# Attention blocks on one core: V weighed one block later, reciprocal sums turned after the projection, their copy after the exponentials

## The reference

```python
q, k, v = proj(Wq), proj(Wk), proj(Wv)           # 16 heads of 32
q, k = _apply_rope(q, cos, sin), _apply_rope(k, cos, sin)
scores = einsum('bhqd,bhkd->bhqk', q, k) / sqrt(32)
scores = where(causal, scores, finfo(float32).min)
attn = einsum('bhqk,bhkd->bhqd', softmax(scores), v)
x = x + layernorm(einsum('bsi,oi->bso', attn, Wo))
# then x = x + layernorm(experts(layernorm(x)))
```

## Time and profile before

| | |
|---|---|
| three runs | 1173.42, 1173.48, 1176.66 us |
| profiled execution: its own time, its span | 1176.2 us, 1174.3 us |
| the attention's blocks | from about 32 to 424 us of the span |
| PE busy over the span | 1080.3 us, 92% |
| DVE, ACT, POOL busy | 683.6, 483.4, 630.4 us |
| granted TensorE clock, mean | 0.975 |

### The profile page before, as it was taken

How to read it: one execution, slowest core, us unless ns; L and a number is a source line. 1 busy time by engine, 2 the same in 40 slices (tenths; PEclk the granted TensorE clock), 3 DMA queues, 4 the chain that set the end, 5 groups by cost and what they waited for, 6 DMA issues and landing times.

```text
span 1174.3 us, 24363 instructions
## 1 busy us (share of the span) xinstructions
PE 1080.3 (92%) x6281; PEld 726.1 (62%) x6282; DVE 683.6 (58%) x2349; ACT 483.4 (41%) x1357; POOL 630.4 (54%) x648
## 2 busy tenths in 40 slices
PE   6999899999999979988879999999999999999973
PEld 3555566555656546555547777777777777767631
DVE  5666566556666668868845444455444444545447
ACT  2666566656666644433212222222222222222223
POOL 3533333333333313321148788888888888888724
PEclk9999999999999999989979999999999999999987
DMA  8700000000000042100259999999999999997796
GB/s 315 287 2 1 3 1 1 2 2 1 1 2 2 1 187 91 63 19 19 72 177 212 222 198 252 248 234 240 260 232 250 243 229 277 272 226 148 110 334 240
DMA packets 66279, 166.71 MB, mean 142 GB/s; under 512 B 15379, under 2 KB 17171, under 8 KB 66081
## 3 DMA queue, kind: packets, MB, share of 16 engines
q0 software_dynamic: 38496, 83.95, 32.6%
q1 hardware_dynamic: 27712, 81.88, 19.7%
HBM read 119.85 MB, written 62.65 MB: 155 GB/s over the span
## 4 chain that ended last, share of the span: by engine, by line
PE 71%; DMA 12%; DVE 6%; issue 4%; ACT 2%; POOL 2%; POOLq 0%; DVEq 0%; SPq 0%; ACTq 0%
PE ps L956 15%; PE ps L700 15%; DMA sum_rows<-x_t,idx 8%; PE ps L967 8%; PE ps L759 6%; PE ps L817 4%; PE ps L729 4%; PE ps L940 4%; PE ps L779 4%; DMA x_t<-x_rows,idx 3%; PE ps L853 3%; PE ps L714 2%; PE ps L869 1%; PE ps L833 1%; POOL x_t L458 1%
## 5 line engine op out<-in xcount | busy, mean ns | idle before, releaser
L956 PE MATMUL ps<-big,work 128*128 x1264 | 300.5, 381 | 0.0
L464 POOL DMA_INDIRECT sum_rows<-x_t,idx x157 | 250.0, 1592 | 52.3 <-issue 40.2
L956 PEld LDWEIGHTS ps<-big,work 128*128 128x128 f32 x1264 | 229.0, 191 | 24.9
L458 POOL DMA_INDIRECT x_t<-x_rows,idx x159 | 166.2, 1045 | 63.5 <-issue 28.1
L700 PE MATMUL ps<-big 128*128 128x384 f32 x512 | 181.5, 499 | 2.1 <-ACT big L533 1.7
L384 POOL TENSOR_TENSOR work<-qkv_all,rope_sb 128x256 f32<-128x256 f32 x64 | 46.7, 729 | 245.2 <-ACT qkv_all L538 245.2
L654 ACT ACTIVATE work<-ps 128x512 f32<-128x512 f32 x159 | 95.0, 597 | 192.6 <-PE ps L940 131.6
L967 PE MATMUL ps<-big,work 128*128 x314 | 161.2, 595 | 1.8 <-issue 1.6
L940 PEld LDWEIGHTS ps<-ident_sb,x_t 128*128 128x128 f32 x636 | 78.7, 142 | 101.6 <-issue 71.0
L1061 DVE CUSTOM_DVE_ANT_0 ps<-ps,mask_sb 128x128 f32<-128x128 f32 (+3 forms) x256 | 120.6, 512 | 23.8 <-PE ps L729 23.0
L557 ACT ACTIVATE work<-ps,neg_max 128x128 f32<-128x128 f32 (+3 forms) x256 | 132.5, 528 | 3.3 <-DVE neg_max L1061 2.4
(11 more groups left out here) (177 smaller groups left out, 1459.9 us busy)
## 6 DMA issues: line engine op xcount, KB each, us to landing
big<-experts SPq DMA_DIRECT2D x65, 768.0 KB, 14.5
sum_rows<-x_t POOLq DMA_DIRECT2D x4, 2048.0 KB
big<-sum_rows SPq DMA_DIRECT2D x8, 768.0 KB, 9.5
x_rows<-work SPq DMA_DIRECT2D x16, 256.0 KB, 2.0
sum_rows<-attn_t POOLq DMA_DIRECT2D x2, 2048.0 KB
out<-x_sb SPq DMA_DIRECT2D x16, 256.0 KB, 5.2
x_sb<-x SPq DMA_DIRECT2D x3, 1024.0 KB, 10.2
x_t<-sum_rows SPq DMA_DIRECT2D x4, 768.0 KB, 13.1
```

The lines of the kernel that those rows point to most:

```text
L458: pool.indirect_dma_start(rows[:, q, :], None, x2_rows, bass.IndirectOffsetOnAxis(ap=idx[:, q, 0:1], axis=0), bounds_check=last_row, oob_i ...
L464: pool.indirect_dma_start(all_sums, bass.IndirectOffsetOnAxis(ap=idx[:, q, 1:2], axis=0), y_sb[:, q, :], None, bounds_check=last_sum, oob_ ...
L956: mm = pe.matmul(ps[:, 2 + p, 0:GATEUP], rows_t[:, p, c, :], w_ring[:, slot, c * GATEUP:(c + 1) * GATEUP], start=(c == 0), stop=(c == DC - 1))
```

## The change

Three things move, on three engines.

- PE: `weigh` of block k-1 now stands in block k between `score` and `xt` or `turn` of head 2. Only the last block of a sequence still weighs at its own end, so that block has two. `turn_rden` stands behind `proj`.
- ACT: `evac_rden` stands behind the exponentials and `evac_qkv`.
- DVE: `weighted` of block k-1 stands in block k behind `evac_pt`, between the second and the third `masked`; block 15's is where it was.

With them the waits change. From block 1 of a sequence on, `qkt` waits for `evac_rden` of the block before (`s_rden_t`), and for `weighted` of the block before that; and `weigh` waits for `take_qkt` of the same block.

```diff
 (ACT)
                     evac_pt(k, i, 2)
-                    evac_rden(k)
                     if i + 1 < BLOCKS or not last:
                         for h in range(HG):
                             exp(b * BLOCKS + (i + 1), (i + 1) % TB, h)
                     if i < BLOCKS - TB or not last:
                         evac_qkv(b * BLOCKS + (i + LEAD_PROJ), (i // TB + 1) % G, i % TB, qkv_bank)
+                    evac_rden(k)
 (PE)
-            def qkt(n, t, k):
+            def qkt(n, t, k, late=False, after=None):
                 pe.wait_ge(s_rope, n + 1)
+                if late:
+                    pe.wait_ge(s_rden_t, k)
+                    if after is not None:
+                        pe.wait_ge(s_attn, after)
...
-                if k is not None and not (isinstance(k, int) and k == 0):
+                if k is not None and not late and not (isinstance(k, int) and k == 0):
                     pe.wait_ge(s_attn, k)
...
-            def weigh(k, i):
+            def weigh(k, i, qkts):
...
                 pe.wait_ge(s_rden_t, k + 1)
+                pe.wait_ge(s_qkt, qkts)
...
                     if i + LEAD_QKT < BLOCKS or not last:
-                        qkt(b * BLOCKS + (i + LEAD_QKT), (i + LEAD_QKT) % TB, k)
+                        qkt(b * BLOCKS + (i + LEAD_QKT), (i + LEAD_QKT) % TB, k, late=(i >= 1),
+                            after=b * BLOCKS + (i - 1) if i >= 2 else None)
                     if i + 1 < BLOCKS or not last:
                         score(b * BLOCKS + (i + 1), (i + 1) % BLOCKS)
+                    if i >= 1:
+                        weigh(b * BLOCKS + (i - 1), i - 1, qkts)
...
                     turn(k, i, 3)
-                    turn_rden(k, b * BLOCKS + min(i + LEAD_QKT + 1, BLOCKS) if last else b * BLOCKS + (i + LEAD_QKT + 1))
                     if i < BLOCKS - TB or not last:
                         proj(b * BLOCKS + (i + LEAD_PROJ), (i // TB + 1) % G, i % TB, qkv_bank,
                              after_xt=(b + 1) * TB if i >= BLOCKS - TB else None)
-                    weigh(k, i)
+                    turn_rden(k, qkts)
+                weigh(b * BLOCKS + (BLOCKS - 1), BLOCKS - 1, qkts)
 (DVE)
                     evac_pt(k, i)
+                    if i >= 1:
+                        weighted(b, b * BLOCKS + (i - 1), i - 1)
                     if more:
                         masked(k1, q1, 2)
                         masked(k1, q1, 3)
-                    weighted(b, k, i)
+                    if i == BLOCKS - 1:
+                        weighted(b, k, i)
```

More of the change, by code:

```diff
@@ L787, in batch @@
                     k = b * BLOCKS + i
+                    qkts = b * BLOCKS + min(i + LEAD_QKT + 1, BLOCKS) if last else b * BLOCKS + (i + LEAD_QKT + 1)
                     turn(k, i, 0)
```

## The result

The changed kernel takes 1196.5 us (median of 6 runs, 1193.7 to 1197.3), the kernel before, run with it, 1174.2 us (6 runs). The ratio is 1.0174, 95% interval 1.0162 to 1.0187, which is 20.4 us (19 to 22); the two medians are 22.3 us apart, and the two profiled executions 20.4 (1196.64 and 1176.2 us). The forecast was +20.7.

The account below looks back on a forecast made before the run. PE was taken to set the pace, by its matmuls plus its standstills. Terms 11.8+3.7+2.2+2.0-1.1+1.0-0.9+2.0 gave +20.7 us on the 1173.5 us median, so 1194 us; own range 1183 to 1206, 8 in 10 1181 to 1207.

Parts of the forecast that it names:

- The main step: At `qkt`, PE newly waits for two queued ACT copies that `weigh` no longer covers; +1.02 us per four blocks in all.
- `norm_x`: On DVE, it follows the reciprocals ahead of `take_qkt` in four blocks of a looped sequence, delaying `weigh`: +2.0 us in all.
- the `xt` terms: At `xt`: its wait hidden by `weigh`, -1.1 us; `proj` behind it losing cover, +1.0; block 15's exponentials, -0.9.
- The prediction's check of blocks 20 to 22: This stretch, 17.23 us before the change, should take 17.8 us after it.
- `weigh` for `take_qkt`: Between `score` and `weigh`: a new wait of 0.17 us with scores of 128 columns, none with 256.
- The shape change: On PE: three tile-shape changes in a block instead of four, saving 0.09 us a block.
- the three sequence ends: Block 15 of each looped sequence: its `weigh` must wait for `evac_rden`, +0.8 us less some hiding, +2.2 in all.
- Behind the last projection: Last four blocks, without projection: `weigh` lies in the chain ahead of `turn`, +2.0 us (-2 to +4).
- The rival of the falling clock: New PE waits lower the clock once in every four blocks: +25 us on top, 1219 us; chance 3%.
- That nothing would replace the wait: At `qkt`, the old wait goes and both ACT copies finish in time: 1159 us; chance 5%.
- That it cancels: PE and ACT react faster than any row shows, leaving about no change: 1171 to 1179 us; chance 6%.
- That the exponentials become the bound beyond qt 3: ACT's exponentials come late by 0.4 us in qt 2 and 0 too: +12, 1206 us and over; chance 9%.

Follow-up runs that it names:

- Experiment 2: The changed kernel with the turned reciprocals in PSUM bank 7, beside the projection, instead of bank 6: 1176.0 us, ratio 1.000 to the kernel before.
- experiment 1: The changed kernel with `evac_rden` ahead of `evac_qkv` on ACT instead of behind it: 1186.8 us, ratio 1.010 to the kernel before.
- experiment 7: The kernel of experiment 2 with `invert` behind `take_qkt` on DVE instead of ahead of it: 1164.3 us, ratio 0.992 to the kernel before.
- experiment 3: The kernel of experiment 2 with `weigh` behind the turns of heads 2 and 3, and `weighted` behind the fourth mask: 1168.0 us, ratio 0.995.
- experiment 6: The changed kernel, reciprocals still in bank 6, with `weigh` behind the turns of heads 2 and 3 and `weighted` behind the fourth mask: 1188.8 us, ratio 1.012.
- experiment 5: The changed kernel with `weigh` back at its own block's end, the moves of `turn_rden` and `evac_rden` kept: 1255.3 us, ratio 1.068 to the kernel before.
- experiment 8: The kernel of experiment 3 with `invert` behind `take_qkt` on DVE: 1166.7 us, ratio 0.993 to the kernel before.
- experiment 9: The kernel of experiment 7 unchanged, measured again in more rounds: 1163.1 us, ratio 0.991 to the kernel before.
- run 10: The kernel of experiment 7 with `weigh` behind the turns of heads 2 and 3 in the last four blocks alone: 1164.5 us, ratio 0.990.
- experiment 4: The changed kernel with `turn_rden` again ahead of `proj` and `evac_rden` ahead of the exponentials, only `weigh` moved: 1194.6 us, ratio 1.017.

## Why the prediction was right, step by step

**The main step** was that `weigh` had covered the copy of the projection on ACT, and that behind it now stands the copy of the reciprocals, for which `qkt` waits because of the bank they share. Experiment 2 takes the shared bank away and with it 22 of 23.4 us of gap, and the loss; experiment 1 shortens the queue ahead of the copy and takes 14.4. So the mechanism is shown. That the total came out within 2 us (+20.7 against 20.4 by the ratio and 22.3 by the medians) is in part luck, as the sum below shows.

**Its sizes.** The waits of `qkt` were forecast at 0.67, 0.45, 0.31 and 0.40 us for qt 0 to 3. The timeline gives 0.63, 0.41, 0.24 (0.20 in the unrolled code), and 0.33 or, at place 7 of a looped sequence, 0.60 (0.24 in the unrolled code). From the scores of block 20 to those of 24 the time grew by 1.00 us (forecast 1.02), but this stretch has place 7 in it; places 1 to 11 together grew by 2.5, which is 0.92 for four blocks. Block by block, from one projection's last record to the next one's, after less before, in the looped sequences (place is the block's number in its sequence: block 19 has place 3):

| block | forecast | measured |
|---|---|---|
| qt 0, places 4 and 8 | +0.16 | +0.10 |
| qt 1, places 1, 5 and 9 | +0.16 | +0.06 |
| qt 2, places 2, 6 and 10 | +0.22 | +0.10 |
| qt 3, place 3 | +0.48 | +0.44 |
| qt 3, places 7 and 11 | +0.48, and `norm_x` at 11 | +0.72 |
| places 12 to 15 together | +1.02, `norm_x`, less 0.3 for the `xt` terms | +0.95 |

The release is seen by PE 0.10 us after the copy ends, not 0.14; that is 0.04 of the differences of 0.06 and 0.10 for qt 0 and 1, and the rest was not traced. The copy of the reciprocals starts 0.10 to 0.12 us before that of the projection is drawn to end, as the forecast's 0.11 has it; the one pair of copies printed in the earlier trace rows (172.52 and 172.95) had shown 0.06. The exponentials do become late in the blocks of qt 3, where the prediction had put it. The rows of block 22 to 23, the place of the earlier trace rows, from P=180.51:

```profile
178.67 0.28 DVE L1091 TENSOR_TENSOR attn_t<-ps,work 128x128 f32 x1
178.87 0.69 DVE L1070 CUSTOM_DVE_ANT_0 ps<-ps,mask_sb 128x512 f32<-128x512 f32 x1
180.01 0.69 ACT L557 ACTIVATE work<-ps,neg_max 128x512 f32<-128x512 f32 x1 [0.38 <-DVE neg_max L1070]
180.51 0.27 PE L772 MATMUL ps<-ident_sb,work 128*128 128x128 f32 x1
181.35 0.49 ACT L538 ACTIVATE qkv_all<-ps 128x384 f32<-128x384 f32 x1
181.72 0.28 ACT L572 ACTIVATE work<-ps 128x128 f32<-128x128 f32 x1
182.10 0.41 PE L718 MATMUL ps<-ident_sb,work 128*128 128x128 f32 x2 [0.45 <-issue]
182.54 0.42 DVE L1024 COPY big<-ps 128x256 f32<-128x256 f32 x1
183.12 0.86 PE L784 MATMUL ps<-x_t,qkv_all 128*32 128x128 f32 x24 [0.18 <-ACT x_t L563]
```

The third mask starts at t+1.65, t being the `turn` of head 2 at 177.22 (forecast 1.67, behind the moved `weighted`). The third exponential starts 1.14 us after its mask, where 0.86 was forecast; `evac_qkv` then starts at P+0.84, not P+0.58. At place 3 the same distance is 0.86, and `evac_qkv` is at P+0.56. The 0.28 more are there at place 7 of each of the three looped sequences and not in the unrolled one. It stays open what they are. At place 11 it is `norm_x` that makes the block longer (next paragraph). The prediction's check of blocks 20 to 22 gives 17.72 us from turn to turn (162.90 to 180.62), 17.8 forecast; 0.22 of its growth is that the stretch now holds `weigh` of blocks 19 to 21 instead of 20 to 22, and 0.27 is what the table has.

**`weigh` for `take_qkt`.** Forecast 0.17 in blocks of qt 3, measured 0.25 (0.34 with the shape change of 0.09). The view names ACT's L563 as what ended it, but these two copies (181.87) belong to block 23, and `weigh` of block 22 doesn't need them; what it needs last is the copy on DVE (L1024), ending at 182.96. `norm_x` makes it 0.53 at place 11, where it precedes. What the prediction didn't see is that this wait was partly hidden by the wait of `qkt`: taken away, `invert` ahead of `take_qkt` costs 10 us more (experiments 2 and 7). In the changed kernel itself these 10 us don't appear.

**The shape change.** Three in a block in place of four, at 0.09: from `score` to `weigh` the shortest gap is 0.087 us. From `weigh` to `turn` the shape costs the same 0.09, and putting `weigh` elsewhere brought a fourth such gap back (experiment 3). So the saving is real, and the forecast's reading of 0.14 as 0.09 and a first load was right.

**The sum.** Up to the last projection the attention grew by 15.9 us: 3.5 in each of the three looped sequences (forecast 4.25, from 3.92, `norm_x` and the `xt` terms), 2.25 for blocks 1 to 11 of the last (forecast 3.45), and 3.2 at the three sequence ends (forecast 2.2). At each end `weigh` starts 0.91 us later against the end of the projection, the moved transpose left out, so 2.7 us are the forecast's term, and the other 0.4 comes of the loop's ends themselves: 0.3 less at the first, 0.7 more at the second, none at the third. At the second the clock stayed low for longer, and a projection there is drawn 4.34 us long instead of 3.21. The low stretch before, and in the changed kernel:

```profile
237.30:240.50 3.20, 3.20 (x15) 1.92 (x16) 1.69 (x7) 1.08 (x5) 0.00 (x0) 0.50 0.00 0
```

```profile
244.50:251.10 6.60, 5.92 (x19) 3.34 (x20) 2.22 (x10) 2.70 (x11) 0.00 (x0) 0.50 0.01 2
```

Behind the last projection the attention grew by 4.1 (forecast 2.2, of which 0.2 for block 12), and by 0.2 ahead of the first. The 4.1 is the term that was sized wrongly most, with two things in it that the prediction didn't have. `turn_rden` of block k waits for `weighted` of block k-1, which stands behind `evac_pt` on DVE; the projection hides this elsewhere, and the last four blocks have none:

```profile
430.12 0.30 PE L772 MATMUL ps<-ident_sb,work 128*128 128x128 f32 x1 [1.03 <-DVE attn_t L1091]
431.92 1.95 PE L733 MATMUL ps<-big 32*128 32x512 f32 x8 [0.82 <-ACT work L557]
433.80 1.08 PE L784 MATMUL ps<-x_t,qkv_all 128*32 128x128 f32 x16
434.81 1.21 PE L763 MATMUL ps<-ident_sb,work 128*128 128x128 f32 x6
```

And the clock fell: these scores of 512 columns are drawn 1.95 us long instead of 1.14, this `weigh` 1.08 instead of 0.64 or 0.65, and the `turn` 1.21 instead of 0.87, 1.6 us in all. The kernel of experiment 1, whose clock stayed at 1.00 there, has 2.4 in place of 4.1; the kernel of experiment 2, whose `turn_rden` doesn't wait for `weighted`, has 0.9. The rival of the falling clock was thus right at two places, which it hadn't named, and wrong for the steady blocks, for which it was priced (146 to 228 us at 1.00).

Together the terms that were too high by 3.5 us (2.3 in the looped blocks, 1.2 in the last sequence) and too low by 3.0 (0.9 at the sequence ends, 1.9 behind the last projection, 0.2 at the start) nearly cancel. About 2.3 of the 3.0 is the lower clock (1.6 and 0.7), which the sum had at nothing: with the clock as it was before, the change would have cost some 18 us, an estimate from these rows. So the sum is nearer than its parts by luck, while the mechanism and the waits, block by block, are not luck.

**The rivals.** That nothing would replace the wait: `qkt` starts at P+0.96 in qt 0. That it cancels: likewise. That the exponentials become the bound beyond qt 3: in qt 2 `evac_qkv` starts 0.25 us after P (174.23 to 174.48, in the profile after) and not later by 0.4; experiment 6 puts all that later exponentials cost at `qkt` at 5 us or less.

## What to carry to other kernels

When work is moved out of a place in which it covered another engine's copies, add up that engine's queue from the moment of its release: here two copies of 0.38 and 0.28 us stood against 0.33 us of cover. Where several results share a PSUM bank and waits keep the engines apart in it, as here, one engine's small copy becomes a wait for unrelated matmuls; moving 128 columns into another bank gave 20 us back. And when a wait is taken away, look at once for the one under it: in this kernel it was a reciprocal ahead of a copy in DVE's queue, worth another 12 us.

## What the runs showed of the hardware

- The granted clock at the end of the attention: in the last four blocks of the changed kernel and of experiments 3 and 5 to 10 a part runs at 0.50 (1.2 GHz; 432.2 to 435.4 us in the changed kernel), in the kernel before and experiments 1, 2 and 4 all of it at 1.00. PE was busy for 4.76 of 7 us in a stretch at 1.00 (the kernel before, 411 to 418) and for 4.70 of 7 in one with the fall in it (run 10, 407 to 414), so these rows don't say why.
- PE stands still at the loop's ends, from the last record of `weigh` to the first `turn` of the next pass: 3.42 and 3.68 us before, 3.46 and 3.32 after, each with a fall of the clock to 0.50 behind it. At the second loop end the changed kernel has 0.50 from 244.5 to 251.1 us, the kernel before from 237.3 to 240.5.
- ACT's third exponential at place 7 of the loop starts 0.28 us later after its mask than the same instruction elsewhere, in all three passes; unexplained.
- Two ACT copies back to back, the projection's and the reciprocals', start 0.37 to 0.39 us apart where the first is drawn 0.49; in the earlier trace rows another pair, with the first drawn 0.49 too, starts 0.43 apart.
